# A table of tile kinds rearranged: three whole tiles a block become VectorE tiles, GpSimd's tiles are spread out, and the product ring has eight slots

## The reference

```python
for idx, (W, b) in enumerate(params):            # 3 layers, W: (39, Fk, 128), Fk = 39, 64, 64
    z = jnp.einsum('bhd,bkd,hks->bsd', x0, xk, W) + b[None, :, None]
    z = jax.nn.relu(z)
    if idx != n_layers - 1:
        half = z.shape[1] // 2
        xk = z[:, :half, :]
        direct.append(z[:, half:, :])
    else:
        direct.append(z)
logit = jnp.sum(jnp.concatenate(direct, axis=1), axis=-1)
```

## Time and profile before

| | |
|---|---|
| median of 3 runs | 1253.2 us (1252.27 to 1253.27) |
| profiled execution, its own time | 1251.91 us |
| span of that execution in the profile | 1250.1 us |
| PE busy | 1182.3 us, 95% |
| DVE busy | 1055.4 us, 84% |
| POOL busy | 1015.9 us, 81% |
| ACT busy | 580.3 us, 46% |

### The profile page before, as it was taken

One profiled execution on the slowest core, in us unless ns is written; L12 is line 12 of the kernel. 1 busy time (PEld: TensorE's weight loads), 2 busy tenths in 40 slices (PEclk: granted clock), 3 DMA queues, 4 the chain that ended last, 5 costly groups with the idle time before them and its releaser, 6 DMA issues.

```text
span 1250.1 us, 14867 instructions
## 1 busy us (share of the span) xinstructions
PE 1182.3 (95%) x3856; PEld 726.7 (58%) x3856; DVE 1055.4 (84%) x919; ACT 580.3 (46%) x563; POOL 1015.9 (81%) x637
## 2 busy tenths in 40 slices
PE   0389999999999999999999999999999999999898
PEld 0155656656565665656566665656566565656565
DVE  2278998989899898989899898989989898999782
ACT  1145454544445444454544444454545444454453
POOL 6778898988888898888889798888989888756661
PEclk9999999999999999999999999999999999999999
DMA  4785626274563627356461635556262745625000
GB/s 124 250 269 187 220 62 224 99 217 164 171 210 99 215 78 236 137 171 210 132 227 60 211 135 186 195 164 217 66 217 101 215 166 171 210 97 165 1 1 1
DMA packets 110269, 196.21 MB, mean 157 GB/s; under 512 B 52975, under 2 KB 64334, under 8 KB 110249
## 3 DMA queue, kind: packets, MB, share of 16 engines
q1 hardware_dynamic: 100009, 193.33, 46.8%
q0 software_dynamic: 10240, 2.64, 1.9%
HBM read 193.36 MB, written 12.78 MB: 165 GB/s over the span
## 4 chain that ended last, share of the span: by engine, by line
PE 67%; POOL 16%; issue 7%; DVE 5%; ACT 3%; DMA 1%; POOLq 0%; DVEq 0%; SPq 0%; ACTq 0%
PE acc L850 65%; POOL lo L465 9%; POOL emb L455 7%; DVE prod L729 2%; ACT hi L588 2%; DVE lo L742 2%; DVE acc L729 1%; DVE hi L739 0%; DMA x_tiles<-x_rows 0%; POOL pairs_r L480 0%; DMA x_rows<-x_rows 0%; PE acc L928 0%; DMA x_rows<-emb 0%; DMA emb<-table,block_idx 0%; DMA base_sb<-base 0%
## 5 line engine op out<-in xcount | busy, mean ns | idle before, releaser
L729 DVE TENSOR_TENSOR prod<-x_tiles,xk 128x1024 f32<-128x1024 f32 (+2 forms) x643 | 757.5, 1215 | 129.6 <-PE acc L850 87.0
L465 POOL TENSOR_TENSOR lo<-prod,hi 128x1024 fp32r<-128x1024 f32 (+1 forms) x288 | 688.8, 2394 | 135.4 <-ACT hi L588 130.6
L850 PE MATMUL acc<-prod,wfull 128*128 128x512 f32 (+2 forms) x1408 | 660.7, 593 | 0.0
L588 ACT ACTIVATE hi<-prod 128x1024 fp32r<-128x1024 f32 (+1 forms) x291 | 308.1, 1060 | 399.6 <-DVE prod L729 316.2
L850 PE MATMUL acc<-hi,whi 128*128 128x512 f32 (+1 forms) x800 | 353.8, 442 | 58.9 <-ACT hi L588 58.9
L850 PEld LDWEIGHTS acc<-prod,wfull 128*128 128x128 f32 (+2 forms) x1408 | 266.4, 189 | 206.0 <-issue 177.7
L455 POOL DMA_INDIRECT emb<-table,block_idx x320 | 308.8, 965 | 69.2 <-issue 62.0
L850 PE MATMUL acc<-lo,whi 128*128 128x512 f32 (+1 forms) x736 | 316.4, 517 | 6.6 <-POOL lo L465 5.4
L850 PE MATMUL acc<-hi,wlo 128*128 128x512 f32 (+1 forms) x800 | 316.5, 396 | 0.0
L850 PEld LDWEIGHTS acc<-lo,whi 128*128 128x128 f32 (+1 forms) x736 | 137.9, 189 | 138.6 <-issue 103.3
L850 PEld LDWEIGHTS acc<-hi,whi 128*128 128x128 f32 (+1 forms) x800 | 151.4, 189 | 114.2 <-issue 70.6
(11 more groups left out here) (73 smaller groups left out, 171.9 us busy)
## 6 DMA issues: line engine op xcount, KB each, us to landing
x_tiles<-x_rows SPq DMA_DIRECT2D x304, 512.0 KB, 5.0
x_rows<-x_rows SPq DMA_DIRECT2D x16, 624.0 KB
x_tiles<-x_rows SPq DMA_DIRECT2D x32, 256.0 KB, 5.6
x_stack<-x_rows SPq DMA_DIRECT2D x48, 156.0 KB
emb<-table,block_idx POOLq DMA_INDIRECT x320, 3.7
x_rows<-emb SPq DMA_DIRECT2D x16, 152.0 KB, 3.3
x_tiles<-w SPq DMA_DIRECT2D x1, 768.0 KB, 6.4
x_tiles<-w SPq DMA_DIRECT2D x1, 704.0 KB, 9.5
```

Source lines behind the costliest of these rows:

```text
L465: nc.gpsimd.tensor_tensor(lo[0:r, product_slot(j), :], prod[0:r, product_slot(j), :], hi[0:r, part_slot(j), :].bitcast(f32), ALU.subtract) ...
L588: nc.scalar.activation(hi[0:r, part_slot(j), :], held(n, parity, j)[0:r, :], ACT.Copy).then_inc(hi_ready, 1)
L729: nc.vector.tensor_tensor(held(n, parity, j)[0:r, :], in0, in1, ALU.mult).then_inc(product_ready, 1)
L850: mm = nc.tensor.matmul(z[:, c], w[0:r], part[0:r, c], start=first and i == 0, stop=last and i == len(weights) - 1)
```

## The change

```diff
-KINDS = ["GFFGFFF", "GFDGF" * 2 + "GFHGF" + "GFDGF", "GFFGF" + "GFFGD" + "GFHGF" + "GFDGF"]
+KINDS = ["GFGFGFF", "GFDGFDGFDGFGHGFDGFDF", "GFGFGFGFGDGFHGFDGFDF"]
 SHORT = 12
...
-PRODS, PARTS = 6, 4
+PRODS, PARTS = 8, 4
```

## The result

The changed kernel takes 1332.15 us (1331.04 to 1333.38, 5 runs) against 1252.46 for the one before: ratio 1.0635, interval 1.062 to 1.0649. It is 80 us slower. The forecast was 1316.5 with a range of 1303 to 1337.

What follows compares the result with a forecast made beforehand. TensorE bounds the kernel, with GpSimd just too late once per step. On 1251.91: -16.3 work, -6.2 old stall, +81.8 new stalls, +1.9 and +2.1 at the ends give 1315.2, with 1.3 to the median 1316.5; range 1303 to 1337.

Steps and rivals of the forecast that it cites:

- The mechanism: GpSimd's chain from layer 0's last G reaches layer 2's fifth G late; TensorE stands still 5.84 us a step, 14 steps.
- the likeliest case: The whole kernel slowed by GpSimd's lateness in layer 2: 1316.5 us, own range 1309 to 1323, chance 0.70.
- rival 1: TensorE's clock falls to 1.2 GHz behind layer 2's 2.48 stall, 1.7 us each, up to 24: 1340, chance 0.10.
- two signs of being wrong: Layer 2's first G starts on GpSimd much before +9.4, or TensorE's clock leaves 1.00 within the steps.
- The chain's start: GpSimd starts layer 0's tile 4 at +4.67 from layer 0's true start, after idling some 4 us.
- 3.6 us of margin at tile 18: Layer 1's D at tile 18: its subtraction, counted from slot release, comes about 3.6 us before TensorE's need.
- The first step: Layer 0 ahead of the steps: three gathers delay GpSimd's third subtraction, and TensorE waits, +1.9 us.
- The end: Last step's layer 1, the G behind `split_top`: chain about 1.1 later, wanted some 1.0 sooner, +2.1 us (0 to 4).
- Costs set at nothing: Three more VectorE subtractions of 1.22 and ScalarE roundings of 1.06 a step fit inside TensorE's time; VectorE 68.4 of 70.4.
- Rivals 2 and 3: GpSimd starts ahead of z1, 1252.7, chance 0.05; the eight slots' lead absorbs layer 2's waits, 1234.7, chance 0.03.
- The step that decides: Layer 2's stall in rival 3: above 1.1 us a step, no gain of 0.2% (2.5 us) is left.
- Rival 2: Layer 0's tile 4 rounded before the relus of z1, a stall of 1.3: no change, 1252.7, chance 0.05.

Runs made afterwards that it cites:

- e3: The changed kernel with layer 2's eight gathers spread one behind each of its eight G tiles, not two behind each of the first four: 1248.07 us, ratio 0.9965.
- e6: The changed kernel with layer 2's table of kinds put back to that of before: 1264.14 us, ratio 1.0092.
- e7: The kernel before with eight product slots and only layer 2's new table of kinds: 1302.81 us, ratio 1.0399.
- e8: e3 with two of layer 0's four gathers moved to layer 1, leaving one behind layer 0's last G: 1230.79 us, ratio 0.9829.
- e2: The changed kernel with six product slots in place of eight, so the new tables alone: 1352.88 us, ratio 1.0808.
- e10: e8 with six product slots in place of eight: 1266.5 us, ratio 1.0107.
- e1: The kernel before with eight product slots in place of six, its tables unchanged: 1247.51 us, ratio 0.9965.
- e4: The changed kernel with the rounding of layer 0's tile 4 ahead of the direct relu of z1 on ScalarE: 1317.3 us, ratio 1.0529.

## Why the prediction was right, and where it was off

**The mechanism** was the forecast's: the waits at layer 2's tiles 4, 6 and 8 in steps 0 to 13, nothing at those places once the gathers are over, a chain in pieces of 4.77 (4.78 forecast), and TensorE alone from there to the next layer 0. The stalls start for start (0.3, 1.7, 1.7, 2.4) stand against 0.0, 1.68, 1.68 and 2.48. e3 removes the gathers from it and the loss goes; e6, e7 and e8 move its start or its deadline, and the steps come out within 0.15 of the sums.

**The difference** between the likeliest case and the measurement is 1332.15 - 1316.5 = 15.6 us: inside the range of 1303 to 1337, which had room for rival 1, but outside the likeliest case's own 1309 to 1323. It has five terms.
- *The clock: +19.2.* This was rival 1, given 0.10, and it came true in twelve of fourteen steps. Its price was right (1.7 forecast, 1.60 measured a fall); the chance was too low. The argument against it, that no row showed what a wait of 2.5 us does, was no evidence against it: the row at hand showed a fall after 3.1 us. One of the prediction's two signs of being wrong, the clock leaving 1.00 within the steps, came true with it: the likeliest case was wrong on the clock.
- *The chain's start: +4.4.* +4.97 and not +4.67, 14 times. The forecast took the relus of z1 to start 0.20 behind layer 0, as before. But the rounding of layer 0's tile 2 stands ahead of them now and waits for VectorE. The statement that GpSimd stands idle for some 4 us before the chain was wrong as well: it is 0.65. Both have one cause, shown by VectorE's rows of the changed kernel, where it works through the end of layer 1 and all of layer 0 without a break:

```profile
490.32 1.22 DVE L729 TENSOR_TENSOR prod<-x_tiles,xk 117x1024 f32<-117x1024 f32 x1
491.46 1.22 DVE L742 TENSOR_TENSOR lo<-xk,hi 128x1024 fp32r<-128x1024 f32 x1
492.59 11.38 DVE L729 TENSOR_TENSOR prod<-x_tiles,xk 117x1024 f32<-117x1024 f32 x10
```

  I had placed its products by when slots come free; here it is its own queue that sets them. The 3.6 us of margin at tile 18 was counted in the same way and was wrong too: VectorE's subtraction for it, at 491.46, ends at 492.68, and TensorE takes it without a wait at

```profile
493.22 0.62 PE L850 MATMUL acc<-lo,whi 128*128 128x512 f32 x2
```

  That is 0.5 us of margin with eight slots, and with six (e2, e10) there is none.
- *The first step: +1.6.* The 1.9 ahead of the steps came as forecast: from layer 0's first matmul to layer 1's it is 71.28 - 51.01 = 20.27 in place of 69.98 - 51.29 = 18.69, so 1.6 more with 0.3 less of work. But in the first step VectorE has no lead yet (it starts layer 1 at 68.92, TensorE at 71.28, and from 71 to 103 it is busy 31.29 of 32.00), and the wait at tile 18 shows once with eight slots as well:

```profile
102.10 0.73 PE L850 MATMUL acc<-lo,whi 128*128 128x512 f32 x2 [1.70 <-DVE lo L742]
```

- *The end: -7.0.* Forecast were +2.1 of waiting and -1.4 of work; from the last start of layer 0 to the end it went from 142.8 to 136.5 us. I looked at one wait of the last step, the one behind `split_top`. It grew from 2.97 to 3.69 by the profile, by starts from 3.1 to (1258.34 - 0.46) - (1253.69 + 0.23) = 3.96, so by 0.9 where I had 2.1. I did not look at the others there: 1.66, 0.56, 1.29 and 1.06 by the profile before, 4.6 in all, and none of them is left. Two of them went with the slots alone in e1.

```profile
1253.69 0.40 PE L850 MATMUL acc<-hi,wlo 128*128 128x512 f32 x1
1257.77 0.73 PE L850 MATMUL acc<-lo,whi 128*128 128x512 f32 x2 [3.69 <-POOL lo L465]
1258.34 0.39 PE L850 MATMUL acc<-hi,whi 128*128 128x512 f32 x1
```

- *The profiled execution: -2.5.* The one of before lay 1.3 under the median of the three runs at hand for the forecast, the one of after 1.2 above its own.

The sum is 19.2 + 4.4 + 1.6 - 7.0 - 2.5 = 15.7. The misses of opposite sign kept it small; the forecast of each of the fourteen steps, 76.24, stands against 77.94 on average. Without the 7.0 at the end, which nothing in the forecast foresaw, the time would have been 1339, above the range. So the mechanism was right, and that the number fell inside was partly luck.

**Costs set at nothing.** VectorE's three operations and ScalarE's three roundings fit in (68.4 of 70.4 forecast, 68.26 of 70.50 in e8), but only with eight slots. The 2.23 for a subtraction with both inputs in SBUF was a mean of two unlike ones, 1.27 and 3.19; the three of the changed kernel took 1.22, 1.51 and 2.19, in sum 0.5 more than before and not 1.0, and no wait of TensorE names them. That the transfers do not matter held in e3 and e8 even with the gathers later.

**Rivals 2 and 3.** The step that decides is 1.1 us of stall. e3, with 1.2 left, came out at 0.9965, just on the fast side. That is because the slots' gain at the end, which the forecast did not have, is in it. Rival 2, the rounding of tile 4 ahead of the relus of z1, was not tried.

**Still open.** Why the clock fell in twelve steps of the changed kernel, in six of e4 and in two of e2, whose waits at layer 2's tiles 4, 6 and 8 are of nearly the same length, and in three of e7 with two such waits; and why it fell behind the wait of 2.97 in the last step of the kernel before and not behind the same wait of 2.99 in e1. So the length of the waits does not decide it alone. The runs show that filling the longest wait removes the falls, and that there are none where these waits are under 1 us (e3, e6).

## What to carry to other kernels

When pieces of work are rearranged over engines, counts and busy shares say little. For each engine that works in a queue, find where its unbroken run starts, what releases it, and when the bottleneck wants its result. A table that spreads one engine's tiles evenly can bunch them against the other work in that engine's queue; here ten gathers stood among six subtractions, and moving them was worth 101 us, while the tables themselves are worth 11.
Where an engine works for a long stretch without a break, as VectorE does here, place its pieces by its own queue, not by when its buffers come free, and price what a wait on the bottleneck does to its clock along with the wait.

## What the runs showed of the hardware

TensorE's granted clock can fall to half (1.2 GHz) after a wait of 2.2 us by the profile that follows two waits of 1.4 within 10 us (12 of 14 steps), or one of 1.4 (3 of 14, e7), not only after one of 3 us: 0.52 over the next 3.4 us, and 1.6 us lost each time. It need not fall after one of 3 us either: behind 2.99 in e1 it was 1.00 over the next 6 us. The Trainium skill (TensorE: Matmul & The Clock Gate, Why this matters for your kernels) warns of gaps above some 3 us between bursts; here shorter ones were enough, and the measurement decides. Eight matmuls with zero weights in the gap kept the clock at full in all fourteen steps, and the kernel with more work was 14 us faster.
